# Twelve tile buffers in place of eight in the expert stage of a fused attention and mixture-of-experts kernel, and pad rows written during attention

## What is computed

```python
def layer(x):
    x = layernorm(x + attention(x))        # 16 heads of size 8, RoPE, causal
    p = softmax(x @ Wg + bg)               # 8 experts
    keep the two largest of p for each token, divided by their sum (+1e-8)
    h = gelu(einsum('bsf,efh->bseh', x, W1) + b1)      # 128 -> 512, tanh form
    y = einsum('bseh,ehf->bsef', h, W2) + b2           # 512 -> 128
    return layernorm(x + einsum('bsef,bse->bsf', y, gates))
```

## Time and profile before

| | us |
|---|---|
| three runs | 836.16, 829.27, 833.98 |
| median | 833.98 |
| the profiled execution, its own time | 828.04 |
| its span in the profile | 825.9 |
| mean granted TensorE clock (share of 2.4 GHz) | 0.912 |

### The profile page before, as it was taken

How to read it: one execution, slowest core, us unless ns; L and a number is a source line. 1 busy time by engine, 2 the same in 40 slices (tenths; PEclk the granted TensorE clock), 3 DMA queues, 4 the chain that set the end, 5 groups by cost and what they waited for, 6 DMA issues and landing times.

```text
span 825.9 us, 19171 instructions
## 1 busy us (share of the span) xinstructions
PE 679.4 (82%) x5560; PEld 362.0 (44%) x5561; DVE 591.8 (72%) x1467; ACT 443.1 (54%) x840; POOL 326.4 (40%) x577
## 2 busy tenths in 40 slices
PE   5858999999988899898889898897879956999830
PEld 2343333333433333334333343332269956989830
DVE  5957788888898988598988889798426721222266
ACT  1323566766546556455556664665736623656524
POOL 3863232243121256322227523134714464444551
PEclk9995699999989899798999999899979977999975
DMA  8767515100101102001011110100167744687924
GB/s 300 254 205 231 141 47 148 47 22 27 47 14 35 37 31 77 27 28 31 17 50 40 58 48 9 39 2 19 35 184 209 197 143 137 179 228 211 304 83 113
DMA packets 72169, 83.71 MB, mean 101 GB/s; under 512 B 9858, under 2 KB 53384, under 8 KB 71952
## 3 DMA queue, kind: packets, MB, share of 16 engines
q1 hardware_dynamic: 67728, 74.04, 30.8%
q0 software_dynamic: 4352, 8.53, 2.9%
HBM read 55.77 MB, written 26.90 MB: 100 GB/s over the span
## 4 chain that ended last, share of the span: by engine, by line
PE 43%; DVE 25%; issue 13%; SPq 8%; ACT 4%; another core or an unknown queue 2%; DMA 2%; POOL 2%; DVEq 0%; ACTq 0%; POOLq 0%
DVE mx L1128 13%; PE banks L722 13%; PE banks L678 9%; PE banks L704 5%; PE banks L780 3%; PE banks L791 3%; SPq L577 2%; PE banks L673 2%; SPq L571 2%; SPq L578 2%; ACT region L836 2%; PE banks L731 2%; DVE w_sb L915 1%; DVE w1e L909 1%
## 5 line engine op out<-in xcount | busy, mean ns | idle before, releaser
L1128 DVE TENSOR_REDUCE mx<-banks 128x1 f32<-128x512 f32 (+3 forms) x640 | 366.4, 631 | 51.4 <-PE banks L678 45.2
L836 ACT ACTIVATE region<-banks 128x1024 f32<-128x1024 f32 (+3 forms) x256 | 201.6, 841 | 164.0 <-PE banks L704 158.7
L678 PE MATMUL banks<-region 64*128 64x512 bf16 (+3 forms) x768 | 197.0, 351 | 18.1 <-DVE mx L1128 16.0
L704 PE MATMUL banks<-region 64*128 64x512 bf16 (+3 forms) x768 | 140.8, 342 | 12.1 <-ACT region L836 6.1
L722 PE MATMUL banks<-region 128*32 128x512 f32 (+3 forms) x1024 | 120.5, 544 | 0.9 <-POOL region L1379 0.8
L836 ACT ACTIVATE cs_sb<-banks 128x1024 f32<-128x1024 f32 (+2 forms) x128 | 91.3, 759 | 41.4 <-PE banks L704 40.6
L1389 POOL DMA_INDIRECT results<-region,dest x72 | 71.9, 999 | 102.5 <-DVE region L1256 74.6
L673 PE MATMUL banks<-mask_sb,half_sb 64*128 64x128 bf16 (+1 forms) x384 | 85.3, 253 | 29.2 <-DVE mx L1128 17.6
L1250 DVE TENSOR_TENSOR region<-banks,w1e 128x128 f32<-128x128 f32 x72 | 21.0, 291 | 109.6 <-PE banks L780 59.4
L1379 POOL TENSOR_SCALAR_AFFINE_SELECT region<-region 128x256 f32<-128x256 f32 x160 | 64.3, 410 | 85.2 <-ACT region L836 82.3
L791 PE MATMUL banks<-region,w1e 128*128 128x128 f32 x576 | 82.8, 290 | 18.4 <-ACT region L862 15.8
(11 more groups left out here) (177 smaller groups left out, 695.8 us busy)
## 6 DMA issues: line engine op xcount, KB each, us to landing
w1e<-in_w SPq DMA_DIRECT2D x72, 322.0 KB
region<-stack SPq DMA_DIRECT2D x128, 56.0 KB
region<-stack SPq DMA_DIRECT2D x64, 112.0 KB
stack<-x_sb SPq DMA_DIRECT2D x16, 384.0 KB, 3.3
region<-pairs SPq DMA_DIRECT2D x72, 66.0 KB
stack<-x_sb SPq DMA_DIRECT2D x16, 256.0 KB, 3.6
region<-results SPq DMA_DIRECT2D x8, 512.0 KB, 4.8
xT_sb<-in_xT SPq DMA_DIRECT2D x4, 512.0 KB, 12.2
```

Source lines behind the costliest of these rows:

```text
L678: last = mm(ring[:, bank, m * n:(m + 1) * n], qst[rows, v % NG, sb_ // 4, slot_, sb_ % 4 * P:(sb_ % 4 + 1) * P], kst[rows, v % NG, slot_, ...
L704: last = mm(score[:, slot_, par, 0:n], kst[rows, u % NG, slot_, j * P:(j + 1) * P], qst[rows, u % NG, c, slot_, s0 - c * CH:s0 - c * CH + ...
L836: nc.scalar.activation(probs[i % 6][:, :, 0:n], score[:, i % 2, :, 0:n], ACT.Exp, scale=SCALE).then_inc(exp_done, 1)
L1128: read(v.tensor_reduce(dst, src, AX.X, ALU.max, negate=True))
```

## The change

`TL` becomes 12: twelve places in `w1e`, `xg`, `ys` and `dest`, and turns of 12 tiles. With it `EARLY` goes from 40 to 36 and `LATE` from 32 to 36; `NTILE` stays 72, `OLD` stays 56 by its own rounding.

Pad rows: the whole region that a batch's rows could reach is filled with pad rows before that batch is scattered. In each of the 16 units SyncE issues two transfers of 1024 rows (528 KB each) behind `MROWS, u, 1`. GpSimd waits for a batch's eight before it scatters the batch. The eight transfers of 66 KB and the reading of `pad_row` go.

SyncE's loads of the expert stage are one loop of 6 turns of 12. At its head it waits for the early words and three batches of scatters, and from turn 3 on for the late words and all scatters. The results of batches 0 to 2 are read by two transfers of 1.5 MB each that ScalarE issues at step 60 (`BACK`, in its walk through the extra events), after the first 56 tiles' results have landed; `FIRST` of any of these batches waits for both. `ys_ready` gets a start of TL, so that the first turn needs no special case.

```diff
-TL = 8
+TL = 12
-OLD = -(-(2 * (B - 1) * BT + E - 1) // TL) * TL
+OLD = -(-(2 * (B - 1) * BT + E - 1) // 8) * 8
...
+    plan[OLD + 4] = [(("BACK",), None)]
     plan[OLD + 9] = [(("FIRST", 0), None)]
...
+            def name_no_place(v, at):
+                b, g = v // NG, v % NG
+                if v == 0:
+                    sp.wait_ge(iota_done, 3)
+                if g == 0 and b > 0:
+                    sp.wait_ge(spare_in, at(16 * 2 * NG * b, 16 * 2 * NG))
+                for e_ in (2 * g, 2 * g + 1):
+                    sp.dma_start(by_expert[e_, bass.ds(at(b * S, S), S), :].rearrange("(t p) n -> p t n", p=P),
+                                 pad[:, :].unsqueeze(1).broadcast_to([P, BT, ROW])).then_inc(spare_in, 16)
...
                     if c == 1:
-                        pass
+                        name_no_place(v, at)
...
-                if not (isinstance(turn, int) and turn == 0):
-                    sp.wait_ge(ys_ready, turn * TL + (k + 1 - TL))
+                sp.wait_ge(ys_ready, turn * TL + (k + 1))
...
             sp.wait_ge(pv_done, NB * (NU - 1))
-            for k in range(TL):
-                load_pairs(0, k)
-            with sp.Fori(1, EARLY // TL - 1) as turn:
+            sp.wait_ge(tiles_spare, 16)
+            with sp.Fori(0, NTILE // TL) as turn:
+                part = (turn + (32 - EARLY // TL)) >> 4
+                sp.wait_ge(tiles_ready, part)
+                sp.wait_ge(pairs_out, part * (16 * 2 * BT) + 16 * 2 * BT * (B - 2))
                 for k in range(TL):
                     load_pairs(turn, k)
-            sp.wait_ge(pad_ready, 1)
-            for e_ in range(E):
-                load_pairs(EARLY // TL - 1, e_)
-                row = sp.value_load(pad_row[0:1, e_:e_ + 1], min_val=0, max_val=(E * CAPT - 1) * P)
-                sp.dma_start(pairs[bass.ds(row, P), :], pad[:, :]).then_inc(spare_in, 16)
-            sp.wait_ge(tiles_ready, 2)
-            sp.wait_ge(spare_in, 16 * (1 + E))
-            sp.wait_ge(pairs_out, 16 * 2 * NT)
-            with sp.Fori(EARLY // TL, NTILE // TL - 1) as turn:
-                for k in range(TL):
-                    load_pairs(turn, k)
-            for k in range(TL):
-                load_pairs(NTILE // TL - 1, k)
-                if k == 1:
-                    for i in range(TL):
-                        sp.wait_ge(result_out[i], 16 * (OLD // TL))
-                if k in (1, 3, 5):
-                    load_back(k // 2)
...
+                elif e[0] == "BACK":
+                    for k in range(TL):
+                        act.wait_ge(result_out[k], 16 * -(-(OLD - k) // TL))
+                    for k in range(2):
+                        act.dma_start(back_old[:, k, :, :], results[k * B * S:k * B * S + (B - 1) * S, :]
+                                      .rearrange("(t p) n -> p t n", p=P)).then_inc(back_in, 16)
...
                     if i == 0:
+                        pool.wait_ge(spare_in, at(16 * 2 * NG * (bt + 1), 16 * 2 * NG))
...
-                    pool.wait_ge(back_in[b], 32)
+                    pool.wait_ge(late_back_in if b == B - 1 else back_in, 32)
...
+            ve.sem_inc(ys_ready, TL)
...
-                pool.wait_ge(ys_ready, turn * TL + (k + 1))
+                pool.wait_ge(ys_ready, turn * TL + (k + 1 + TL))
```

More of the change, by code:

```diff
@@ L365, in build @@
         yb = region[:, 3328:3584].rearrange("p (b n) -> p b n", b=2)
-        ys = region[:, 3584:4608].rearrange("p (b n) -> p b n", b=TL)
-        back = [region[:, 4608 + i * 2 * BT * D:4608 + (i + 1) * 2 * BT * D].rearrange("p (k t n) -> p k t n", k=2, n=D)
-                for i in range(B)]
+        ys = region[:, 3584:3584 + TL * D].rearrange("p (b n) -> p b n", b=TL)
+        back_old = region[:, 5120:5120 + 2 * (NT - BT) * D].rearrange("p (k t n) -> p k t n", k=2, n=D)
+        back = [back_old[:, :, b * BT:(b + 1) * BT, :] for b in range(B - 1)]
+        back.append(region[:, 5120 + 2 * (NT - BT) * D:5120 + 2 * NT * D].rearrange("p (k t n) -> p k t n", k=2, n=D))
         stats = sb("stats", [P, BT, 6])
@@ L434, in build @@
         spare_in = sem("spare_in")
-        pad_ready = sem("pad_ready")
+        tiles_spare = sem("tiles_spare")
         tiles_ready = sem("tiles_ready")
@@ L447, in build @@
         result_out = [sem(f"result_out{k}") for k in range(TL)]
-        back_in = [sem(f"back_in{k}") for k in range(B)]
+        back_in = sem("back_in")
+        late_back_in = sem("late_back_in")
         first_added = sem("first_added")
@@ L565, in visit @@
                         sp.dma_start(pairs[E * CAPT * P:, :].rearrange("(t p) n -> p t n", p=P),
-                                     pad[:, :].unsqueeze(1).broadcast_to([P, SPARE, ROW])).then_inc(spare_in, 16)
+                                     pad[:, :].unsqueeze(1).broadcast_to([P, SPARE, ROW])).then_inc(tiles_spare, 16)
             walk(sp, visit)
@@ L607, in _ @@
             for k in range(TL):
-                load_pairs(NTILE // TL - 1, k)
-                if k == 1:
-                    for i in range(TL):
-                        sp.wait_ge(result_out[i], 16 * (OLD // TL))
-                if k in (1, 3, 5):
-                    load_back(k // 2)
-            for k in range(TL):
                 sp.wait_ge(result_out[k], 16 * (NTILE // TL))
-            load_back(B - 1)
+            for k in range(2):
+                sp.dma_start(back[B - 1][:, k, :, :], results[k * B * S + (B - 1) * S:(k + 1) * B * S, :]
+                             .rearrange("(t p) n -> p t n", p=P)).then_inc(late_back_in, 16)
             for b in range(B):
```

7 lines of the change are left out of this document (1 added, 6 removed).

## The result

The changed kernel takes 847.46 us (median of 4 executions, 836.75 to 855.44), the kernel before beside it 835.07 (4 executions, 829.27 to 836.6). The ratio is 1.0119, 95% interval 1.0064 to 1.0173; it leaves out the execution of 855.44, which is a slow one and lengthens the median. So the change makes the kernel slower, by 1.2% or about 10 us, where 826 had been forecast. The profiled execution took 847.78 us, 19.7 more than the one of before.

A forecast was written before the change was run, and what follows sets the result against it. The prediction took VectorE and TensorE to bound attention, SyncE's loads the late expert stage, late signals the scatters; -11.0 + 1.0 + 1.6 + 0.5 = -7.9 us from 833.98 gave 826 us, range 812 to 842 (own range 820 to 831).

The forecast's parts named there:

- Pads during attention: Attention: 32 pad transfers of 528 KB cost 0, since traffic there is low and the engines looked undisturbed.
- Rival 1: Attention: pads stall engines through late signals; 44 us, 870, or 8 us if only three units with scatters suffer; chance 0.14.
- Results read back by ScalarE: Expert stage, step 60: ScalarE's two issues lose 1.0 us (bounds 0 and 3), late data 1.6 us (bounds 0 and 8).
- The wait for the data: End of expert stage: `FIRST` of batch 0 waits for all 3 MB of results, 1.6 us lost.
- Rival 2: Late expert stage: reads return at 166 GB/s, 19 us, beside the last loads; gain lost, 834; chance 0.17.
- The lead over tiles 36 to 71: Expert stage: loads run ahead, TensorE becomes the bound at 1.98 us a tile, 11.0 us gained.
- The loop of loads: Head of SyncE's load turns: register waits and sum delay tile 0 by 0.5 us; later the lead hides it.
- The burst of scatters: Batch 3's scatters, 656 to 700 us: their 25 us loss stays, 0 change, bounds -20 and +12.
- The end: Last transpose to last scatter of results: 8.9 us, left unchanged.
- rival 3: Batch 3's scatters: the burst shrinks too, 10 to 20 us more gained, 811; chance 0.18.
- rival 4: Batch 3's scatters: the burst grows with 12 tiles in flight, +12 us, 838; chance 0.07.

The follow-up runs named there:

- e11: Changed kernel, pads still in attention, results of batches 0 to 2 read by SyncE in three 1 MB pieces between its last loads; 836.57 us, ratio 1.0007.
- e3: Changed kernel with the pads as before: none in attention, eight of 66 KB by SyncE behind the loads of tiles 28 to 35; 834.87 us, ratio 0.9989.
- e9: Changed kernel with the eight late pads of before and SyncE reading results in three 1 MB pieces behind the loads of tiles 69 to 71; 825.08 us, ratio 0.991.
- e1: Kernel before with the 32 pad transfers of attention added, its own late pads kept; 840.68 us, ratio 1.0061.
- e6: Kernel before with batch 3's sixteen scatters one a step, at steps 18 to 33, instead of two; 830.75 us, ratio 0.9981.
- e2: Changed kernel with a batch's eight pad transfers in its units 0, 1 and 2, none in the unit with scatters; 842.52 us, ratio 1.0092.
- e5: Changed kernel with all six expert-stage turns written out on TensorE, ScalarE, VectorE and GpSimd; 841.63 us, ratio 1.0124.
- e4: Changed kernel with the results of batches 0 to 2 read by SyncE after its last tile load instead of by ScalarE; 845.45 us, ratio 1.0136.
- e7: Changed kernel with late pads by SyncE as before and the results of batches 0 to 2 read by SyncE after its last load; 831.75 us, ratio 1.0015.

## Why the prediction was wrong

Three terms of the sum against what the runs give. With ScalarE's read taken out, the changed kernel goes from 1.0119 to 1.0007 (e11) and e3 from 0.9989 to 0.991 (e9): 0.8 to 1.1%, 7 to 9 us. With the pads taken out, it goes from 1.0119 to 0.9989 (e3) and e11 from 1.0007 to 0.991: 1.0 to 1.3%, 8 to 11 us. What is left is -0.9%, -7.5 us (e9). Each difference has 0.5 to 0.7 per cent of uncertainty. They are steps on one way from before to the changed kernel, so that they add up to the +1.2% is no proof of them.

**"Pads during attention ... 0".** This is the step that failed, and it decides the sign. I had read that the one pad transfer of this form leaves the engines at their work, that the fortieths of attention have traffic to spare, and that this was the nearest row. All of that holds for the windows of that one transfer, and none of it says anything on a late signal, which was what the earlier trace rows showed beside heavy traffic. The measured price beside twelve buffers is 8 to 11 us, 0.25 to 0.34 us for each of the 32 transfers (in the kernel before, e1, 5 to 6 us), and it comes in few places: 7.4 us in unit 7 and 1.8 in unit 1 of the profiled execution. Unit 11 has most of its 5 us with and without pads (33.3 to 33.5 in e3, e6 and e9, 29.2 in the trace of before); it goes with the granted clock, which in that unit was 1.00 in the trace of before and 0.90 in those of e3 and e9. So of the 17.9 us of attention some 13 are the pads' even there.

Rival 1 was this mechanism, with 0.14. Its smallest case, 8 us from three units with scatters, has the size by luck; it had no chance of its own, and its condition was wrong, since e2 keeps a ratio of 1.0092 with no pad in the scatters' units. What holds a signal back for 5 us isn't shown by any row. The place doesn't explain it either: the eight loads behind the pads of unit 7 took SyncE 8.55 us to issue, but they took 7.75 before, and 8.81 in e5, both without the hole.

**"Results read back by ScalarE", 1.0 + 1.6 us.** 7 to 9 us, and all of it in the first term. The two issues were put at 0.5 us each, from SyncE's transfers of 0.5 MB, with an upper bound of 3. The first took 0.85, the second 5.65 (6.92 in e3's trace), and ScalarE's copy for the next tile stands behind it. Behind the gap TensorE ran at a granted clock of 0.50. From tile 60 to 71 that makes 29.4 us against the 21.4 of e4 and e11. What should have warned me is the size: each transfer is three times what the row showed. Whether the size or the loads in flight make the issue long, no run separates; the engine doesn't, by e4 and e7.

The wait for the data, my 1.6 us, did not come. The first and the last addition of results in the changed kernel, and the last in the kernel before:

```profile
804.76 2.39 POOL L1372 TENSOR_TENSOR x_sb<-x_sb,region 128x1024 f32<-128x1024 f32 x1
...
827.33 2.37 POOL L1372 TENSOR_TENSOR x_sb<-x_sb,region 128x1024 f32<-128x1024 f32 x1 [5.04 <-DMA region<-results]
```

```profile
806.93 2.34 POOL L1372 TENSOR_TENSOR x_sb<-x_sb,region 128x1024 f32<-128x1024 f32 x1 [4.76 <-DMA region<-results]
```

Batch 0's starts right behind a scatter; the wait of 5.04 us is batch 3's, which the kernel before has too. The last packets of ScalarE's queue end between 802 and 803 us, 18 us after the issue at 784.41, so the 3.1 MB came at about 170 GB/s. Rival 2 had this right, 19 us at 166 GB/s, and its effect wrong: the data were in time only because the tiles had been held up by 8 us. Where they weren't, in e4, batch 0's addition waits 5.39 us.

The Trainium skill, page "DMA: Bandwidth & Descriptors", section "Issuing engines are not separate DMA queues", says that starting transfers on another engine saves only the sequencer's time. The trace agrees that no bandwidth was won. While most of the reads ran, the core moved 291 GB/s in the changed kernel, first row, and 315 in the kernel before, second row:

```profile
784.40:801.10 16.70, 11.65 (x80) 11.46 (x80) 3.06 (x15) 6.26 (x24) 4.65 (x5) 0.80 0.97 291
```

```profile
767.00:785.00 18.00, 15.27 (x128) 14.25 (x127) 4.87 (x21) 9.79 (x39) 9.26 (x8) 1.00 1.05 315
```

The same section calls that time "usually small relative to the DMA itself"; here it was 6.5 of 18 us, on an engine on the path.

**"The lead over tiles 36 to 71", -11.0.** The mechanism was right in part: SyncE left the chain, the loads are 12 us ahead, and e9's stretch from tile 36 to 71 takes 73.1 us where the kernel before took 80.3, so -7.2. Where it comes from was not what I wrote. The 2.90 us a tile at the end became 1.90, 6.3 us from tile 63 on. The 2.2 in the middle stayed: the loop's 1.98 is right as a median (2.02), but I had counted nothing for single long distances (2.7, 2.8 and 3.7 us in place of 2.0 at tiles 51, 56 and 58, in e9 too), only one of which is behind a late signal. The row behind it, one distance of two transposes, is a best case and not a mean. The 4.2 to 5.4 us that I took for a landing are those of batch 3's two reads alone, at 801 us, with nothing beside them; with the loads 12 us ahead that did no harm.

**"The loop of loads", 0.5.** From the last exponential to tile 0 it is 1.2 us more, 9.5 against 8.3, both in the changed kernel and in e9. Mis-sized by 0.7.

**"The burst of scatters", 0; "The end", unchanged.** Tiles 22 to 31 took 0.8 us less, so neither rival 3, which needed 10 to 20 us less, nor rival 4, which needed 12 more, came. The end is 1.2 us longer, 10.1 against 8.9.

Put together: a lead of -7.5 with the loop's head, the reads +8, the pads +9 to +11. Without the two added costs, the forecast of 826 would have been near (825.08 in e9), and in part by luck: the lead was too large by 3.8 us in that sum, and the reads' 2.6 us stood against it.

## What to carry to other kernels

Extra DMA traffic in a phase that looks idle for the DMA engines is not free for that reason: ask what signals its engines live on, and put the traffic alone into the old kernel before building on it. A wait of TensorE can cost more than its own length: look at the granted clock behind it. When a wait is taken off one queue, look for the work that came to another one with it: a large DMA issued by an engine on the path is a stall of that engine, and one issued too late is a wait where its data are needed. e9 keeps both away with three smaller reads by SyncE, placed where the loads are well ahead. Take a stage's pace from many distances and not from the best one.

## What the runs showed of the hardware

- Signals that the profile can lay to no instruction came up to 5.4 us late in unit 7, and not in the traffic's peak but behind it. The DMA rates of 300 to 330 us in the changed kernel, in fortieths of 0.75 us, show 244 to 303 GB/s from 315 to 319.5 us; TensorE stands from 321.0 to 326.67, at 60 to 153 GB/s:

```profile
GB/s 0 0 0 0 90 0 0 90 11 0 106 0 6 90 0 11 0 90 19 8 258 271 303 294 284 244 163 179 122 83 129 60 153 75 114 127 22 123 57 131
```

- After 5.67 us of idle TensorE in unit 7 the granted clock was 0.50 from 324 to 332 us; after the gap at tile 63 it was 0.50 from 790.7 to 797.4. In both stretches TensorE was busy again before the clock came back.
- The second of two transfers of 1.5 MB that one engine issues one behind the other held ScalarE for 5.65 us (6.92 in e3) and SyncE for 5.05 and 3.13 (e4, e7); the first held them for 0.80 to 1.08.
- The late signals around a burst of 16 scatters sum to the same, 47.1 and 46.3 us in one trace each, whether two or one go out in a step.
- The same matmuls in a loop over a register come 2.02 us a tile, written out 1.90.
